# Where the keys and values of a second attention are projected: behind the first attention in fp32, or behind the first expert layer in split fp16

## What is computed

```
x = x + tanh(g_xattn[0]) * attention0(layernorm(x), ctx)      # one head of 256
x = x + tanh(g_ffn[0])   * experts0(layernorm(x))             # 8 experts, the best 2 of each token
x = x + tanh(g_xattn[1]) * attention1(layernorm(x), ctx)      # 16 heads of 64
x = x + tanh(g_ffn[1])   * experts1(layernorm(x))             # each of 8 experts takes 256 tokens
# attention1:  k = ctx @ Wk (192 x 1024),  v = ctx @ Wv (192 x 1024)
#              softmax(q k' / 8) v, then @ Wo + bo
```

## Time and profile before

| what | us |
|---|---|
| median of 3 runs (1504.62 to 1508.01) | 1505.31 |
| the profiled execution's own time | 1509.33 |
| its span in the trace | 1507.4 |
| TensorE busy | 1287.9 (85%) |
| VectorE busy | 961.0 (64%) |
| ScalarE busy | 642.5 (43%) |
| GpSimd busy | 630.0 (42%) |

### The profile page before, as it was taken

How to read it: one execution, slowest core, us unless ns; L and a number is a source line. 1 busy time by engine, 2 the same in 40 slices (tenths; PEclk the granted TensorE clock), 3 DMA queues, 4 the chain that set the end, 5 groups by cost and what they waited for, 6 DMA issues and landing times.

```text
span 1507.4 us, 30560 instructions
## 1 busy us (share of the span) xinstructions
PE 1287.9 (85%) x9764; PEld 972.5 (65%) x9765; DVE 961.0 (64%) x2090; ACT 642.5 (43%) x2032; POOL 630.0 (42%) x643
## 2 busy tenths in 40 slices
PE   6866179999999988999999920389999999999995
PEld 3655168899999956788888810146665556665554
DVE  2887336655555576789888789476556666556550
ACT  3775024333333265888888730133233333233220
POOL 2277736666666530545454430312223322233213
PEclk8675579999999989999999965699999999999998
DMA  4556126543343340010101120322333333332212
GB/s 146 200 163 188 29 50 130 85 67 60 66 63 63 56 127 1 15 36 28 35 28 35 36 98 0 105 77 70 109 74 78 84 77 71 110 71 39 32 15 28
DMA packets 75076, 107.14 MB, mean 71 GB/s; under 512 B 20278, under 2 KB 66876, under 8 KB 71932
## 3 DMA queue, kind: packets, MB, share of 16 engines
q0 software_dynamic: 29312, 37.31, 15.4%
q1 hardware_dynamic: 44700, 68.62, 14.2%
q10 hardware_dynamic: 992, 0.27, 0.1%
HBM read 69.65 MB, written 36.52 MB: 70 GB/s over the span
## 4 chain that ended last, share of the span: by engine, by line
PE 73%; issue 10%; DVE 6%; DMA 4%; ACT 3%; POOL 2%; SPq 0%; another core or an unknown queue 0%; ACTq 0%; POOLq 0%; DVEq 0%
PE psG L122 6%; PE psU L123 6%; PE psU L122 6%; PE psU L124 6%; PE psG L124 6%; PE psG L123 6%; PE psYb L122 4%; PE psYb L124 4%; PE psYb L123 4%; PE psS L122 2%; PE psS L123 2%; PE psS L124 2%; PE psP L1412 2%; PE psY L122 2%; PE psY L123 2%
## 5 line engine op out<-in xcount | busy, mean ns | idle before, releaser
L1705 POOL DMA_INDIRECT out_x<-yo,gidx x64 | 101.9, 1592 | 337.9 <-ACT yo L1787 323.3
L1817 DVE SCALAR_TENSOR_TENSOR hid<-psU,sil 128x512 f32<-128x512 f32 x128 | 88.5, 692 | 187.5 <-ACT sil L1776 185.7
L922 POOL DMA_INDIRECT x_rows<-yo,tabs x78 | 125.1, 1604 | 108.8 <-ACT yo L985 91.5
L1776 ACT ACTIVATE sil<-psG 128x512 f32<-128x512 f32 x128 | 76.4, 597 | 204.2 <-PE psU L124 195.6
L1359 ACT ACTIVATE pr<-psS,mx 128x77 f32<-128x77 f32 x512 | 158.3, 343 | 5.9 <-DVE mx L1491 4.0
L122 PE MATMUL psYb<-W1h,hh 128*128 128x256 f16 x512 | 139.6, 273 | 1.8 <-ACT yo L1787 1.8
L123 PE MATMUL psYb<-W1l,hh 128*128 128x256 f16 x512 | 139.6, 273 | 0.0
L124 PE MATMUL psYb<-W1h,hl 128*128 128x256 f16 x512 | 139.6, 273 | 0.0
L1012 DVE SCALAR_TENSOR_TENSOR hid<-psU,sil 128x512 f32<-128x512 f32 x78 | 53.9, 691 | 129.2 <-ACT sil L976 128.6
L1359 ACT ACTIVATION_READ_ACCUMULATOR pr<-psS,mx 128x1 f32 x512 | 114.9, 224 | 0.0
L122 PE MATMUL psG<-gxh,W1h 128*128 128x512 f16 x256 | 97.7, 382 | 7.8 <-DVE gxl L1808 5.5
(11 more groups left out here) (324 smaller groups left out, 4053.4 us busy)
## 6 DMA issues: line engine op xcount, KB each, us to landing
w1s<-in_w SPq DMA_DIRECT2D x16, 1536.0 KB, 6.3
stage<-in_w SPq DMA_DIRECT2D x8, 1536.0 KB
X<-in_x SPq DMA_DIRECT2D x8, 512.0 KB, 8.8
n_rows<-xc SPq DMA_DIRECT2D x8, 512.0 KB
x_rows<-X SPq DMA_DIRECT2D x8, 512.0 KB
X<-x_rows SPq DMA_DIRECT2D x8, 512.0 KB, 8.2
out_x<-X SPq DMA_DIRECT2D x32, 128.0 KB, 1.7
n_rows<-xn SPq DMA_DIRECT2D x32, 128.0 KB, 1.8
```

The lines of the kernel that those rows point to most:

```text
L922: pool.indirect_dma_start(x1_rows[:, :], bass.IndirectOffsetOnAxis(tabs[:, j, n, 0:1], 0), yo[:, par, n, :], None, compute_op=ALU.add).the ...
L1705: pool.indirect_dma_start(out_rows[:, :], bass.IndirectOffsetOnAxis(gidx[:, half, col:col + 1], 0), yo1[:, j % 2, n, :], None, compute_op= ...
L1776: act.activation(sil1[:, f % 2, :], psG1[f % 2][:], ACT.Silu, scale=1.0 / (SX * SW)).then_inc(d_sil, 1)
L1817: dve.scalar_tensor_tensor(hid1[:, f % 2, :], psU1[f % 2][:], SH / (SX * SW), sil1[:, f % 2, :], ALU.mult, ALU.mult).then_inc(d_hid, 1)
```

## The change

The two projections leave stage 3 and stage 2's pieces, and stand at the end of stage 1. Raw fp32 weights and context are loaded into the two halves of `stage`, the buffer through which the expert weights have come, and are multiplied as fp32: two products (128 and 64 rows deep) for each of 16 outputs. `K1` lies beside the expert layer's tiles; `V1` and `V2` lie in the memory of `X`, whose rows have been stored by then, and the second attention works on a new tile `X2`. The zeros are now written by ScalarE (`K1`, `V1`) and VectorE (`V2`). Of the five pieces two stay, `wq1` and `wo1`.

```diff
+        def project_pe(pe):
+            pe.wait_ge(u_w, 6 * 16)
+            pe.wait_ge(s_exp, NG)
+            pe.wait_ge(s_ptl, NG)
+            pe.wait_ge(s_res, GT * NG)
+            for n, raw in enumerate((rawk, rawv)):
+                for m in range(HP):
+                    o = psK[m % 4]
+                    wait(pe, u_pl, HP * n + m - 3)
+                    for rows, k in ((P, 0), (DC - P, 1)):
+                        at = k * H * DH + m * P
+                        last = pe.matmul(o, raw[0:rows, at:at + P], rawc[0:rows, k * NKEY:(k + 1) * NKEY],
+                                         start=(k == 0), stop=(k == 1))
+                    last.then_inc(u_p, 1)
+
+        def project_act(act):
+            act.wait_ge(s_slot, NG)
+            act.wait_ge(s_wt, 4 * NG)
+            act.wait_ge(s_blk, 15)
+            act.wait_ge(s_keep, 16 * NG)
+            act.wait_ge(u_z, 1)
+            for i in range(2):
+                act.activation(K1[i][DH:P, :, 0, :].bitcast(F32), nil[DH:P, :].unsqueeze(2).to_broadcast([DH, HP, NKEY // 2]), ACT.Copy)
+                ins = act.activation(K1[i][0:DH, :, 1, :].bitcast(F32), nil[0:DH, :].unsqueeze(2).to_broadcast([DH, HP, NKEY // 2]), ACT.Copy)
+            for m in range(HP):
+                act.wait_ge(u_p, m + 1)
+                for odd, rows in enumerate(halves):
+                    ins = act.activation(K1[0][rows, m, odd, :], psK[m % 4][rows, :], ACT.Copy, scale=SK)
+                ins.then_inc(u_ph, 1)
+            for v in V1:
+                v32 = v.rearrange("p m b k -> p (m b k)").bitcast(F32)
+                act.activation(v32, nil[:, 0:1].to_broadcast([P, VN // 2]), ACT.Copy).then_inc(u_z, 1)
...
+            for m in range(HP):
+                act.wait_ge(u_p, HP + m + 1)
+                for odd, rows in enumerate(halves):
+                    act.activation(V1[0][rows, m, :, odd * KM:(odd + 1) * KM], keys_of(psK[m % 4], rows, 0, KM), ACT.Copy, scale=SK)
+                    ins = act.activation(V2[0][rows, m, :, in_v2(m, odd)], keys_of(psK[m % 4], rows, KM, KR), ACT.Copy, scale=SK)
+                ins.then_inc(u_ph, 1)
+
+        def project_dve(dve):
+            for m in range(HP):
+                dve.wait_ge(u_ph, m + 1)
...
+                if m == 1:
+                    dve.wait_ge(s_keep, 16 * NG)
+                    for v in V2:
+                        last = dve.memset(v.bitcast(F32), 0.0)
+                    last.then_inc(u_z2, 1)
...
@@ attn0_sync
+            sp.wait_ge(s_wl, 2 * (E - 1))
+            for src, dst, cols in (("wk1", rawk, H * DH), ("ctxT", rawc, NKEY)):
+                sp.dma_start(dst[:, 0:cols], a[src][0:P, :]).then_inc(u_w, 16)
+                sp.dma_start(dst[0:DC - P, cols:2 * cols], a[src][P:DC, :]).then_inc(u_w, 16)
+            sp.wait_ge(s_wl, 2 * E)
+            sp.dma_start(rawv[:, 0:H * DH], a["wv1"][0:P, :]).then_inc(u_w, 16)
+            sp.dma_start(rawv[0:DC - P, H * DH:2 * H * DH], a["wv1"][P:DC, :]).then_inc(u_w, 16)
             store_rows(E - 1)
...
-        PIECES = [("ctx1", "ctxT", NKEY, SK), ("wk1", "wk1", H * DH, SW), ("wv1", "wv1", H * DH, SW),
-                  ("wq1", "wqT1", D, SW), ("wo1", "wo1", D, SW)]
+        K1 = [sb(f"K1{part}", [P, HP, 2, NKEY], F16, r2, "right") for part in "hl"]
+        PIECES = [("wq1", "wqT1", D, SW), ("wo1", "wo1", D, SW)]
...
@@ gather of ffn0_gpsimd, up of ffn0_tensor
+                wait(pool, u_p, HP if j == 0 else 0)
...
+                        wait(pe, u_pl, 2 * HP if isinstance(j, int) and j == 0 else 0)
...
+        rawk, rawc = stage[:, 0, 0:2 * H * DH], stage[:, 0, 2 * H * DH:2 * H * DH + 2 * NKEY]
+        rawv = stage[:, 1, 0:2 * H * DH]
+        psOf = psO[:].rearrange("p i d -> p (i d)")
+        psK = [psS[:, 0:NKEY], psP[:, 0:NKEY], psOf[:, 0:NKEY], psOf[:, 512:512 + NKEY]]
...
@@ prep_sync
-                sp.dma_start(X[:, GT * g:GT * g + GT, :], x1v[:, GT * g:GT * g + GT, :]).then_inc(u_x, 16)
+                sp.dma_start(X2[:, GT * g:GT * g + GT, :], x1v[:, GT * g:GT * g + GT, :]).then_inc(u_x, 16)
...
@@ prep_gpsimd goes; prep_tensor, prep_scalar and prep_vector lose their loops over m for K1, V1, V2
+                    if b == 0 and m == 0:
+                        pe.wait_ge(b_yo, NB0)
```

More of the change, by code:

```diff
@@ new lines, in project_dve @@
+        def project_dve(dve):
+            for m in range(HP):
+                dve.wait_ge(u_ph, m + 1)
+                for odd, rows in enumerate(halves):
+                    ins = dve.scalar_tensor_tensor(K1[1][rows, m, odd, :], psK[m % 4][rows, :], SK, K1[0][rows, m, odd, :],
+                                                   ALU.mult, ALU.subtract)
+                ins.then_inc(u_pl, 1)
+                if m == 1:
[3 more added lines that the diff above has]
+                    last.then_inc(u_z2, 1)
+            for m in range(HP):
+                dve.wait_ge(u_ph, HP + m + 1)
+                for odd, rows in enumerate(halves):
+                    part = slice(odd * KM, (odd + 1) * KM)
+                    dve.scalar_tensor_tensor(V1[1][rows, m, :, part], keys_of(psK[m % 4], rows, 0, KM), SK,
+                                             V1[0][rows, m, :, part], ALU.mult, ALU.subtract)
+                    part = in_v2(m, odd)
+                    ins = dve.scalar_tensor_tensor(V2[1][rows, m, :, part], keys_of(psK[m % 4], rows, KM, KR), SK,
+                                                   V2[0][rows, m, :, part], ALU.mult, ALU.subtract)
+                ins.then_inc(u_pl, 1)
@@ L833, in program @@
         r2 = ExitStack()
[L834 to L836 removed]
+        K1 = [sb(f"K1{part}", [P, HP, 2, NKEY], F16, r2, "right") for part in "hl"]
+        PIECES = [("wq1", "wqT1", D, SW), ("wo1", "wo1", D, SW)]
+        tiles_of = {"wq1": HP, "wo1": HP}
         split1 = {name: [sb(f"{name}{part}", [P, tiles_of[name] * cols], F16, r2, "right") for part in "hl"]
@@ L1097, in prep_sync @@
             sp.dma_start(N1[HP * KR:HP * KR + 1, :, HP, :], bo4[:].rearrange("p b a d -> p b (a d)").to_broadcast([1, B, 2 * D])).then_inc(u_n1, 16)
-        def prep_gpsimd(pool):
-            pool.wait_ge(b_y, NB0)
-            for i in range(2):
-                pool.memset(K1[i][DH:P, :, 0, :].bitcast(F32), 0.0)
-                pool.memset(K1[i][0:DH, :, 1, :].bitcast(F32), 0.0)
-                pool.memset(V1[i][DH:P, :, :, 0:KM].bitcast(F32), 0.0)
-                pool.memset(V1[i][0:DH, :, :, KM:P].bitcast(F32), 0.0).then_inc(u_z, 1)
         def prep_tensor(pe):
-            cth, ctl = split1["ctx1"]
+            wqh, wql = split1["wq1"]
+            woh, wol = split1["wo1"]
             pe.wait_ge(b_w1h, len(PIECES))
             pe.wait_ge(b_w1l, len(PIECES))
-            for m in range(HP):
-                if m == 2:
-                    pe.wait_ge(b_yo, NB0)
-                for turn, (name, psum) in enumerate((("wk1", psM), ("wv1", psN))):
-                    wh, wl = split1[name]
-                    o = psum[m % 4][:, :] if psum is psM else psum[m % 4][:, :, :].rearrange("p a d -> p (a d)")
-                    wait(pe, u_pl, 2 * (m - 4) + turn + 1)
-                    for rows, k in ((P, 0), (DC - P, 1)):
-                        at = k * H * DH + m * P
-                        last = mm3(pe, o[:, 0:NKEY], wh[0:rows, at:at + P], wl[0:rows, at:at + P],
-                                   cth[0:rows, k * NKEY:(k + 1) * NKEY], ctl[0:rows, k * NKEY:(k + 1) * NKEY], k == 0, k == 1)
-                    last.then_inc(u_p, 1)
             pe.wait_ge(u_pl, 2 * HP)
-            wqh, wql = split1["wq1"]
-            woh, wol = split1["wo1"]
-            pe.wait_ge(u_z, 2)
             for b in range(B):
@@ L1441, in run @@
                 def run(t, par):
[L1442 removed]
+                    row = X2[:, bass.ds(t, 1), :].rearrange("p t d -> p (t d)")
                     if n == 1:
```

73 lines of the change are left out of this document (19 added, 54 removed).

## The result

The changed kernel takes 1500.24 us (median of 7 runs, 1497.30 to 1504.98), the kernel before 1508.01 us (7 runs, 1504.62 to 1508.94). The ratio is 0.9949, 95% interval 0.9934 to 0.9965: faster by 0.5%, where 1.8% was forecast. The profiled execution took 1500.24 us.

What follows compares the result with a forecast made beforehand. VectorE's remainders were taken to bound prep, TensorE the part after, and GpSimd's scatter, table load and gather to fill the hole. -24.4 - 3.8 + 1.5 = -26.7 from 1505.3 gave 1478.6 us; range 1474 to 1487.

Steps and rivals of the forecast that it cites:

- What goes from prep: Between the first expert layer and the M1 products: 21.6 us of remainders vanish, 2.8 more from full clock; -24.4 us.
- What goes from the expert layer: First expert layer: with two pieces only the second can meet the single-buffer wait; -3.8 us, bounds -1.9 and -5.7.
- What comes between attention and experts: Hole before the first gate product: projections delay it 3.6 us to 202.8, warm gate products give back 2.1; net +1.5 us.
- TensorE is warm for the values: Value projections before the gate product: full clock after unbroken work from about 183, 0.52 us a product; net +1.5 us.
- the bound of +11.4: Hole before the experts: at 1.32 us a product with cold values, the gate product starts at 212.7; net +11.4 us.
- The rival with a thin cover: Late last store, slowed scatters or slow X2 reloads; store at 176 instead of 170.9 gives +5, 1483.7 us; chance 0.06.
- The +1.5: Stretch between attention and experts: gate product 3.6 us later, less 2.1 us for gate products at full clock.
- its cold case: Hole before the experts: values at half clock, 2.06 us each output, gate product at 206.9; net +5.6 us.
- The rule that was weighed: TensorE's clock in the projections: bursts with waits between drop the clock repeatedly; if PSUM waits count, values cold, +5.6 us.
- the values run cold: Rival for the value projections: half clock costs +5.6 to +11.4 instead of +1.5; 1482.7 to 1488.5 us; chance 0.22.
- three signs of being wrong: Before the experts: first zero fill after 174, value products keeping 1.03 us, or first transposes waiting for a key-delayed gather.
- The slower rival, a ring that collapses: Projections before the experts: engines take turns for each output, gate product near 249, +50, time 1525 us; chance 0.03.

Runs made afterwards that it cites:

- eight areas: Changed kernel with eight PSUM areas in turn instead of four for the key and value outputs: 1496.14 us, ratio 0.9897 to the kernel before.
- the run with the burst ahead of the keys: Changed kernel with eight PSUM areas and 24 unused fp16 products right behind the last ranks, ahead of the keys: 1495.37 us, ratio 0.9898.
- The four runs with it: Changed kernel, early 24 fp16 products, eight PSUM areas, plus slot tables and copies first (1494.78), copies first (1494.31), slot tables (1494.61), or both and store first (1497.21 us).
- the two with the burst behind the scatters: Changed kernel with eight PSUM areas and 24 unused fp16 products between keys and values: 1492.41 us; the same with four key copies before the fills: 1492.27 us.

## Why the prediction was off

The forecast was 1478.6 us and the measured time 1500.24 us. The mechanism was right in two of its three terms, and the third took back most of what they gave.

**What goes from prep: right.** -24.4 forecast, -24.60 measured, with the clock at 1.00 from the first window. The reloads of `X2` stayed hidden.

**What goes from the expert layer: right.** -3.8 forecast, -4.57 measured; one piece meets its wait, as foretold.

**What comes between attention and experts: wrong.** +1.5 forecast, +22.0 measured. This is the step that failed, in its numbers and in one assumption.

- The assumption that TensorE is warm for the values. It rested on prep, where the clock rose within 5.6 us of unbroken work. Those were fp16 products. Here 26 us of unbroken fp32 products, and 42 with eight areas, left it at 0.50, so it was not the waits. The same fp32 products, with the same copies beside them, kept full clock for 11 us once fp16 products had raised it. That it is fp32 as such is not shown: at the start of the kernel fp32 products, all 128 rows deep, raised it.
- The size of a product. 1.03 us was taken at half clock; it is 1.32. The first of the earlier trace rows had this very value (6.48 to 7.81) and the same shape, 128 and 64 rows in turn; I chose one between the later, shorter rows of 1.1 and 0.89, which belong to products that are all 128 rows deep and in which the clock rose, and kept 1.32 only for the bound of +11.4. The Trainium skill, page "FP8 and Floating Point Precision", section "TensorE Precision Notes", counts four passes for true fp32. Four times 308 columns at 1.2 GHz would be 1.03 us by estimate. The trace agrees for the products that are 128 rows deep (two instructions 0.51 us apart); the alternating ones take 1.32, at full clock 0.67 to 0.71. Why alternating costs 0.3 us more, no run shows.
- ScalarE's start. 170.9 was taken from the block table of the kernel before, 178.30 was measured. The rival with a thin cover named one of its two causes (the store late behind the 768 KB) and priced it at +5. It missed that the scatters land 7.1 us later beside those loads, so that the block table is late by as much. There were 8.1 us of pauses; eight areas ended them and shortened the distance by 6.0.
- A credit that was not due. The +1.5 is 3.6 for the later gate product less 2.1 for gate products at full clock. The clock was at 0.50 up to 224 and at 0.88 in 224 to 228, so the 2.1 did not come. The prediction took them off in its cold case too, where TensorE is cold at that point by its own condition: +5.6 and +11.4 should read +7.7 and +13.5, and the rival's 1482.7 to 1488.5 should be 1484.8 to 1490.6.

TensorE's own account gives the whole: 167.34, 16 outputs at 2.65 (42.4), pauses of 7.12 and 1.02, and 3.3 from the last product to the gate product make 221.2. Without the pauses it would be 213.1, close to the 212.7 that the prediction had for 1.32 us a product, and 213.1 - 199.17 = 13.9 of the 22.0 us are what the projection costs with fp32 at half clock; the other 8.1 are the pauses. The rule that was weighed, of bursts with waits that drop the clock (the Trainium skill, page "TensorE: Matmul & The Clock Gate", section "HAM oscillation — how this bites in real kernels"), gave the better answer, cold values, but not for the reason that it names: without any waits they were cold too. In the run with the burst ahead of the keys its mechanism did show, when a wait of 4.56 us ended the full clock.

**The rival "the values run cold"** is what happened, and it took the late start besides, so the time, 1500.24, lies above its upper end of 1488.5 and outside the range. Of the prediction's three signs of being wrong two came: the first zero fill after 174 (178.30), and value products that stay slow (1.32 us). The third did not: the first gather did wait for the keys (197.69 instead of 192.42), but the transposes at 217.97 follow the last product without a pause. The slower rival, a ring that collapses, did not come about: TensorE had two pauses, not one for each output.

**Open.** Why signals of TensorE's keys reached ScalarE some 17 us after the recorded products when a burst stood ahead of them, and whether it is the scatters beside them. The four runs with it and the two with the burst behind the scatters, without it, fit that, but no run took the scatters away, since the expert layer reads what they write. Also open is why these fp32 products leave the clock low when those at the start of the kernel raised it. Nor was it tested whether real fp16 work in the burst's place would do as well.

## What to carry to other kernels

A projection moved into a hole costs what its slowest resource does there, not where it came from: take the price of an fp32 product from a row at the clock that the hole has, and from a row of the same shape; and don't count on unbroken work to raise the clock until a row shows work of that kind doing it. If fp16 products stand nearby, put such work right behind them. When loads are moved up, look at which small transfers share the DMA engines with them, and who waits for those.

## What the runs showed of the hardware

- Unbroken work did not always raise TensorE's clock: fp32 products of 308 columns, 128 and 64 rows deep in turn, left it at 0.50 in 42.4 us without a pause, and held 1.00 for 11 us after 24 fp16 products had raised it. At the start of the kernel fp32 products that were all 128 rows deep raised it, at 15.9 us.
- Such a product took 1.32 us at half clock and 0.67 to 0.71 at full clock when the depths alternated, 1.03 us at half clock when all were 128 rows deep; the alternating one with bf16 operands took 0.37 at half clock.
- Full clock, 1.00 while TensorE worked, was gone after a wait of 4.56 us (0.60 in the window in which it began again).
- The wait for GpSimd's scatters of slots took 8.66 us beside loads and a store of some 1.8 MB in 160 to 172, and 1.79 us without them.
- In four runs with 24 fp16 products ahead of the keys, while GpSimd issued scatters, TensorE's signals reached ScalarE up to 17 us behind the recorded products. The cause is open.
